# Last FFN stage: the shifted values and the final adds on GpSimd, both PSUM halves scaled by ScalarE

## What is computed

```python
def _L1_ffn_ref(x, weight):
    x_scale = 448.0 / max(abs(x))
    w_scale = 448.0 / max(abs(weight))
    x_fp8 = clip(x * x_scale, -448, 448).astype(float8_e4m3fn)
    w_fp8 = clip(weight.T * w_scale, -448, 448).astype(float8_e4m3fn)
    return (x_fp8 @ w_fp8.T) * (1 / x_scale / w_scale)
...
x = x + tanh(g_ffn[1]) * _L1_ffn_ref(layernorm(x), L1_ffn_weight)
```

## Time and profile before

| what | value |
|---|---|
| median of 3 runs | 1390.06 us (1390.04 to 1390.81) |
| profiled execution's own time | 1390.46 us |
| its span in the profile | 1388.6 us |
| busy share PE / PEld / DVE / ACT / POOL | 96 / 77 / 64 / 50 / 25 % |
| last stage | from about 1309.6 us of the span to its end |
| granted TensorE clock, mean | 0.994 of full |

### The profile page before, as it was taken

How to read it: one execution, slowest core, us unless ns; L and a number is a source line. 1 busy time by engine, 2 the same in 40 slices (tenths; PEclk the granted TensorE clock), 3 DMA queues, 4 the chain that set the end, 5 groups by cost and what they waited for, 6 DMA issues and landing times. The chain is left out here.

```text
span 1388.6 us, 26402 instructions
## 1 busy us (share of the span) xinstructions
PE 1329.8 (96%) x10067; PEld 1062.4 (77%) x10067; DVE 892.8 (64%) x1444; ACT 688.1 (50%) x1762; POOL 347.7 (25%) x403
## 2 busy tenths in 40 slices
PE   6999999999999999889999999999989999998798
PEld 6999889999999999757888888888854544554544
DVE  4452468778787786754232346659756688885897
ACT  4222067787777777863111201013326666665396
POOL 0000024132231240110110204214233444443224
PEclk9999999999999999999999999999999999999999
DMA  6752563755647538755545445112246444444123
GB/s 227 240 177 81 138 171 99 204 144 135 178 129 197 166 102 204 152 173 171 188 168 179 169 147 202 37 54 69 81 106 143 106 105 105 105 106 91 62 106 137
DMA packets 138321, 192.74 MB, mean 139 GB/s; under 512 B 31815, under 2 KB 101575, under 8 KB 137312
## 3 DMA queue, kind: packets, MB, share of 16 engines
q1 hardware_dynamic: 138208, 191.16, 47.5%
HBM read 95.92 MB, written 35.29 MB: 94 GB/s over the span
## 5 line engine op out<-in xcount | busy, mean ns | idle before, releaser
L1276 ACT ACTIVATE a_prob<-a_psS,a_negmax 128x256 f32<-128x256 f32 x512 | 237.7, 491 | 91.2 <-DVE a_negmax L1166 90.6
L998 PE MATMUL a_psQ<-a_xT_hi,wide 128*128 128x256 f32 x912 | 174.5, 290 | 0.8 <-POOL a_xT_lo L946 0.8
L1166 DVE TENSOR_REDUCE a_negmax<-a_psS 128x4 f32<-128x1024 f32 x128 | 153.5, 1200 | 25.6 <-PE a_psS L1022 25.3
L1504 PE MATMUL m_psY<-wide,m_a_hi 128*128 128x512 f32 x512 | 158.0, 390 | 0.3 <-DVE m_a_lo L1554 0.3
L1504 PE MATMUL m_psY<-w_ffn,m_a_hi 128*128 128x512 f32 x512 | 158.3, 390 | 0.0
L1293 ACT COPY a_probT<-a_psT 128x512 f32<-128x512 f32 x208 | 115.5, 606 | 55.7 <-PE a_psT L1031 55.6
L998 PEld LDWEIGHTS a_psQ<-a_xT_hi,wide 128*128 128x128 f32 x912 | 138.7, 189 | 1.1 <-POOL a_xT_lo L946 1.1
L1031 PE MATMUL a_psT<-ident,a_prob 128*128 128x128 f32 x1024 | 133.4, 273 | 0.0
L998 PE MATMUL a_psQ<-a_xT_lo,wide 128*128 128x256 f32 x456 | 127.6, 280 | 0.0
L1031 PEld LDWEIGHTS a_psT<-ident,a_prob 128*128 128x128 f32 x1024 | 115.2, 141 | 0.9 <-issue 0.8
L1276 ACT ACTIVATION_READ_ACCUMULATOR a_prob<-a_psS,a_negmax 128x1 f32 x512 | 113.7, 222 | 0.0
(11 more groups left out here) (260 smaller groups left out, 2729.9 us busy)
## 6 DMA issues: line engine op xcount, KB each, us to landing
a_q_stack<-a_q_hi SPq DMA_DIRECT2D x128, 128.0 KB, 3.0
a_q_stack<-a_q_lo SPq DMA_DIRECT2D x128, 128.0 KB, 2.6
b_q_stack<-b_q_hi SPq DMA_DIRECT2D x128, 128.0 KB, 2.4
c_raw<-lay_ctxT SPq DMA_DIRECT2D x16, 512.0 KB, 4.6
rows<-in_x SPq DMA_DIRECT2D x8, 1024.0 KB, 5.3
scratch_o<-rows SPq DMA_DIRECT2D x16, 512.0 KB, 3.1
m_x<-in_x SPq DMA_DIRECT2D x8, 1024.0 KB, 5.7
scratch_x<-m_x SPq DMA_DIRECT2D x8, 1024.0 KB, 5.1
```

The lines of the kernel that those rows point to most:

```text
L998: last = nc.tensor.matmul(bank[:, 0:S], w[:, kt, t * P:(t + 1) * P], a[:, u, kt, :], start=(kt == 0 and w is wq.hi and a is xT_hi), stop=( ...
L1166: nc.vector.tensor_reduce(negmax[:, n % 2, :], psS[:, bank:bank + 2, :].rearrange("p a (j k) -> p (a j) k", k=S), AX_X, ALU.max, negate=Tr ...
L1276: last = nc.scalar.activation(prob[:, n % 2, j, :], psS[:, 2 * (n % 2) + j // 2, (j % 2) * S:(j % 2 + 1) * S], ACT.Exp, bias=negmax[:, n % ...
L1504: last = nc.tensor.matmul(psY[:, 2 * t + h, :], a[:, u, kt, rows_t], m[:, kt, cols], start=(kt == 0 and a is a_hi and m is w.hi), stop=(kt ...
```

## The change

ACT no longer writes `shifted`: POOL makes it from `scaled` by a multiplication with 2^20 (`tensor_scalar`, 128x1024 float32). DVE no longer finishes the right half: ACT scales it out of PSUM as it does the left one (`scale_right`, behind `scale_left`), and POOL adds the rows to it. POOL's list is now shift(0), shift(1), and then for each k: shift(k+2), left add of k, right add of k. PE's wait for the right buffer is on ACT's `right_scaled`.

```diff
         @block.gpsimd
         def _(pool):
             nc.gpsimd.tensor_copy(ident16[:, :], sh.ident[:, :]).then_inc(ident_ready, 1)
+
+            def shift(k):
+                pool.wait_ge(scaled_ready, k + 1)
+                if k >= AHEAD:
+                    pool.wait_ge(magic_ready, k - AHEAD + 1)
+                nc.gpsimd.tensor_scalar(shifted[:, k % AHEAD, :], scaled[:, k % AHEAD, :], FP8_SHIFT, None, ALU.mult
+                                        ).then_inc(shifted_ready, 1)
+
+            shift(0)
+            shift(1)
             for k in range(TILES):
-                left = slice(0, HALF_N)
-                pool.wait_ge(left_scaled, k + 1)
-                nc.gpsimd.tensor_tensor(y[:, k % Y_SLOTS, left], y[:, k % Y_SLOTS, left], rows_of(k, left), ALU.add
-                                        ).then_inc(left_ready, 1)
+                if k + 2 < TILES:
+                    shift(k + 2)
+                for half, (half_scaled, half_ready) in enumerate(((left_scaled, left_ready), (right_scaled, right_ready))):
+                    cols = slice(half * HALF_N, (half + 1) * HALF_N)
+                    pool.wait_ge(half_scaled, k + 1)
+                    nc.gpsimd.tensor_tensor(y[:, k % Y_SLOTS, cols], y[:, k % Y_SLOTS, cols], rows_of(k, cols), ALU.add
+                                            ).then_inc(half_ready, 1)
...
                 if k >= 2:
-                    pe.wait_ge((left_scaled, right_ready)[h], k - 1)
+                    pe.wait_ge((left_scaled, right_scaled)[h], k - 1)
...
-            def finish_right(k):
-                right = slice(HALF_N, D)
-                dve.wait_ge(psY_full, 2 * k + 2)
-                if k >= Y_SLOTS:
-                    dve.wait_ge(y_stored[k % Y_SLOTS], 16 * (k // Y_SLOTS))
-                nc.vector.scalar_tensor_tensor(y[:, k % Y_SLOTS, right], psY[:, k % 2, 1, :], out_scale[:, 0:1], rows_of(k, right),
-                                               op0=ALU.mult, op1=ALU.add).then_inc(right_ready, 1)
-
...
                 round_tile(k)
-                if k >= 2:
-                    finish_right(k - 2)
-            for k in range(TILES - 2, TILES):
-                finish_right(k)
...
-                for m, dst, ready in ((1, shifted, shifted_ready), (0, scaled, scaled_ready)):
-                    nc.scalar.activation(dst[:, k % AHEAD, :], rows_of(k), ACT.Identity, bias=offset[:, m, b, t:t + 1],
-                                         scale=factor[:, m, b, t:t + 1]).then_inc(ready, 1)
+                nc.scalar.activation(scaled[:, k % AHEAD, :], rows_of(k), ACT.Identity, bias=offset[:, 0, b, t:t + 1],
+                                     scale=factor[:, 0, b, t:t + 1]).then_inc(scaled_ready, 1)
...
+            def scale_right(k):
+                act.wait_ge(psY_full, 2 * k + 2)
+                nc.scalar.mul(y[:, k % Y_SLOTS, HALF_N:D], psY[:, k % 2, 1, :], out_scale[:, 0:1]).then_inc(right_scaled, 1)
...
                 if k + 1 < TILES:
                     copy_transposed(k + 1)
                 scale_left(k)
+                scale_right(k)
```

More of the change, by code:

```diff
@@ L2419, in ffn1_stage @@
         psT_full, xqT_ready, psY_full = sem("psT_full"), sem("xqT_ready"), sem("psY_full")
+        right_scaled = sem("right_scaled")
         left_scaled, left_ready, right_ready = sem("left_scaled"), sem("left_ready"), sem("right_ready")
```

## The result

| | before | changed |
|---|---|---|
| median | 1390.43 us | 1489.81 us |
| runs | 4, 1390.04 to 1392.49 | 4, 1488.69 to 1491.94 |
| span of the profiled execution | 1388.6 us | 1486.9 us |
| its own time | 1390.46 us | 1488.73 us |

The ratio is 1.0705, with a 95% interval of 1.0693 to 1.0718: slower, as forecast, but by 98.3 us on the span where the prediction had 62.8 us, and above its range.

A forecast was written before the change was run, and what follows sets the result against it. PE bounds the last stage without gaps, 3.90 us per tile. 1390.46 us plus 51.5 (ring) and 1.3 (tail), 52.8 together, gives 1443.3; plus 10 for the clock, 1453 us; range 1441 to 1475 us.

The forecast's parts named there:

- The ring: Last stage: shift(k+3) waits behind tile k's adds, delaying transposes; 7.86 us per tile against 3.90, 13 times, 51.5 us.
- the price of the shift: POOL's 128x1024 multiplication by a constant, taken as 1.04 us like the one-input cast; each 0.1 us more costs 1.3 us.
- the two-input end: Rival: POOL's shift costs 2.54 us like a two-input add; 19.5 us more, 1473 us; chance 0.15.
- The rest of the ring: Waits between successive transposes besides the shift: 2.32 us to the adds, adds 2.54, magic 0.60, xq 1.21, handoffs 0.05 and 0.10.
- The clock: PE idles 3.96 us per ring, falling to 1.2 GHz in 6 of 13: 10 us; always-full-clock rival 1443 us, chance 0.2.
- A ring slowed throughout: One turn with PE at half clock: right add late, 9.61 us, 1.75 us more than at full clock.
- The head: Before the first transposes: weight's landing covers the first shifts, xq(0) ready about 1318.2 us, 0.6 us ahead; T(1) stays.
- The tail: After the last product: ACT's eviction, handoff and POOL's add take 2.08 us instead of DVE's 0.04 + 0.75; adds 1.3 us.
- So the two do not disturb each other: DVE's total falls when POOL is idle, so it takes 1.22 us instead of the mean 1.56.
- The rule of the Trainium skill: Rival price for POOL's shift: about 1.8 cycles per element, 1.54 us; 6.5 us more, 1460 us; chance 0.15.

The follow-up runs named there:

- order alone: Changed kernel with POOL's shift of tile k+3 put ahead of the two adds of tile k, same work; 1435.1 us, ratio 1.0327.
- The copy: Changed kernel with POOL's multiplication by 2^20 replaced by a plain copy of the same 128x1024 tile, factor left out; 1455.85 us, ratio 1.0461.

## Why the prediction was wrong, point by point

- **The ring** was right, in its members, their order and their number: T(1) to T(14), 13 times, then one period that PE sets. Loosened by order alone it gives back 55 us.
- **The step that failed is the price of the shift**, "it has one input, as the cast has, so I take 1.04 us". It is 2.77 us, which is even above the upper end of 2.54 us, "the two-input end". 13 x 1.73 = 22.5 us of the 35.5 us that were missed. The copy, which does take 1.04 us, brings the kernel to 1455.85 us against the forecast 1453. Number of inputs was the wrong likeness: the row that I took as the bound was for another kind of instruction, not for a dearer one. The shift alone would have brought the forecast to 1453 + 22.5 = 1475.5 us, the edge of the range; the clock, the head and the tail took it beyond.
- The rest of the ring: 7.86 + 1.73 = 9.59 us forecast, 9.67 measured. 1 us in all.
- **The clock**: that it falls in the idle stretches was right, the count was not. "About every second ring, 6 of 13: 10 us"; it was 12 of 13, partly or wholly, and 17.3 us. A ring slowed throughout was worked out as 9.61 us, with the measured shift 11.34; the longest are 11.36 us. The count rested on a recovery behind an idle stretch of 1.6 us. Ahead of the transposes that end the rings of 11.36 us, TensorE stood idle for 4.4 to 4.9 us, as the shift was longer. But the shift is not the whole reason: with the copy of 1.04 us, too, 12 of 13 rings were longer than at full clock, each by less than the forecast's 1.75 us, and their 11.6 us lie near the forecast's 10 us by luck.
- **The head**, "xq(0) is ready at about 1318.2 us, 0.6 us ahead" of the weight: it held T(0) back by 3.1 us. Three shifts of 2.8 to 3.3 us stand in a row there, and they collide with `magic` and `xq`. With the copy 1.2 us of it stayed, so the forecast's "0.6 us ahead" left out the collisions as well.
- **The tail**: 1.3 us forecast, 3.0 measured. The T(14) to T(15) period ran for the most part at half clock (5.58 us, not 3.90); the part behind the last product is the 1.3 us.
- "So the two do not disturb each other", said of `total` and GpSimd, holds in the ring (1.22 and 1.26 us), but not in the head and not once the ring is loosened. It cost the changed kernel little, and it took from the repairs tried here what their sums had promised.
- The rule of the Trainium skill that the prediction weighed (GPSIMD Engine Reference, Performance versus the Vector engine; 1.54 us by my estimate) is stated as a best case, and as a price it misses both ways: the shift took 2.77 us, the copy 1.04; the two-input form took 1.90.

How most of the collisions look fits another page's sentence. The Trainium skill (SBUF — State Buffer, "SBUF: two separate sides") says that the port pair shared by the two engines "is an **exclusive lock**, not a bandwidth split", held for the whole instruction by whoever starts first. `magic` beside an add, 1.79 us and ended 0.56 us behind the add's end, agrees with that. `magic` beside the second shift of the head does not: it began 0.03 us behind the shift and ended 1.2 us before it. For the `tensor_scalar` form "the whole instruction" is not what this trace shows. The lock as such no run shows.

No variant beat the kernel before, nor did any show whether another repair could. TensorE has no idle time in its last stage there, so freed time on ScalarE and VectorE had nothing to buy; the best one with the full output was 1403.99 us.

## What to carry to other kernels

When work moves to an engine that follows its own list, write down what stands ahead of each new instruction and whether that waits, by way of others, for what the new instruction makes: sums per tile (3.6 us under 3.9 us here) say nothing about such a ring, and every member of it is paid in full each time. Take a price only from a row of the same kind of instruction (a cast is no arithmetic, even with the same shapes and inputs), and where there is none let the range reach well beyond the nearest rows. An idle stretch on TensorE costs again through its clock, and GpSimd and VectorE durations taken from a trace in which the two never meet are lower ends.

## What the runs showed of the hardware

- GpSimd, 128x1024 float32, undisturbed: copy 1.04 us; multiplication by a constant 2.77, by a scalar from SBUF 2.84; two-input multiplication by a repeated column 1.90; two-input add 2.54. One input more made the multiplication cheaper.
- GpSimd against VectorE, whichever starts first keeping its time beside an add: a 128x1024 two-input VectorE operation of 1.22 us took 2.29 us beside a pair of GpSimd adds, `magic` 1.66 to 1.79 us instead of 0.69, the pair of adds 3.76 us instead of 2.5. Beside a shift of 2.77 us a `magic` took 1.55 us and ended before the shift, and a `total` took 1.23 us as if alone.
- TensorE's clock: with idle stretches of 4.4 to 5.6 us in rings of 9.7 to 11.4 us the granted clock was 0.77 in the mean; with the idle stretch filled by transposes it was 1.00, and the kernel 18.7 us faster. With the copy (rings of 7.9 to 9.5 us) it was 0.79.
